# A selective scan: the velocity made for two values of n per weight load, and the work on it ordered by pairs of n

## The reference

```python
xz = einsum("bld,ed->ble", x, in_w); xb, z = split(xz)
xb = silu(causal_conv4(xb) + cb)
delta, Bm, Cm = split(einsum("ble,re->blr", xb, xp_w))     # 16, 16 and 16 columns
delta = softplus(delta @ dtw.T + dtb)
dA = exp(delta[..., None] * -exp(a_log))
mi = delta[..., None] * Bm[:, :, None, :] * xb[..., None]
# over time, for every channel e and state n:
v = 0.6 * v + mi_t
h = dA_t * h + v
y_t = sum over n of h * C_t
# and then
out = einsum("bld,ed->...", (y + dp * xb) * silu(z), ow)
```

## Time and profile before

| | us |
|---|---|
| runs | 4443.35, 4444.9, 4454.01 |
| median | 4444.9 |
| profiled execution, its span | 4448.6 |
| TensorE busy (PE) | 3574.1, 80% |
| VectorE busy (DVE) | 2793.3, 63% |
| ScalarE busy (ACT) | 1980.3, 45% |
| GpSimd busy (POOL) | 2081.9, 47% |

### The profile page before, as it was taken

One profiled execution on the slowest core, in us unless ns is written; L12 is line 12 of the kernel. 1 busy time (PEld: TensorE's weight loads), 2 busy tenths in 40 slices (PEclk: granted clock), 3 DMA queues, 4 the chain that ended last, 5 costly groups with the idle time before them and its releaser, 6 DMA issues. The chain is left out here.

```text
span 4448.6 us, 88475 instructions
## 1 busy us (share of the span) xinstructions
PE 3574.1 (80%) x28540; PEld 2392.4 (54%) x28541; DVE 2793.3 (63%) x4863; ACT 1980.3 (45%) x4454; POOL 2081.9 (47%) x1206
## 2 busy tenths in 40 slices
PE   6888869936988889888875888888988884499980
PEld 4454546624555555555543555555555553388870
DVE  3444432345777777777755777777777776655545
ACT  1212112205656666566634666656666553233320
POOL 0101000014667666676652766667667675422216
PEclk8888878967999999999986999999999995599995
DMA  1000000011313222132221221312223224211113
GB/s 50 0 0 0 0 21 0 0 56 41 74 51 73 52 54 74 49 75 52 53 63 33 64 61 51 76 50 60 66 51 73 51 55 152 99 48 47 47 40 109
DMA packets 151619, 230.36 MB, mean 52 GB/s; under 512 B 25106, under 2 KB 83890, under 8 KB 149556
## 3 DMA queue, kind: packets, MB, share of 16 engines
q1 hardware_dynamic: 143156, 202.30, 17.1%
q0 software_dynamic: 8064, 23.08, 1.8%
HBM read 119.99 MB, written 23.59 MB: 32 GB/s over the span
## 5 line engine op out<-in xcount | busy, mean ns | idle before, releaser
L893 POOL TENSOR_TENSOR m_hc<-m_h,m_Cb 128x1024 f32<-128x1024 f32 x512 | 1204.9, 2354 | 766.3 <-DVE m_h L1014 446.9
L1014 DVE TENSOR_TENSOR_SCAN m_h<-m_dA,m_hlast,m_bank 128x256 f32<-128x256 f32 x2048 | 1354.3, 725 | 145.3 <-PE m_bank L1295 62.6
L1277 PE MATMUL m_bank<-m_hc,ident 128*128 128x512 f32 x2048 | 1210.2, 680 | 147.9 <-POOL m_hc L893 147.6
L1144 ACT ACTIVATE m_dA<-m_delta,m_rate 128x256 f32<-128x256 f32 x2048 | 894.1, 500 | 16.3 <-DVE m_h L1014 15.4
L1293 PEld LDWEIGHTS m_bank<-m_M,m_U 128*128 128x128 bf16 x8192 | 605.1, 101 | 362.4 <-DVE m_h L1014 223.8
L1293 PE MATMUL m_bank<-m_M,m_U 128*128 128x64 bf16 x8192 | 675.2, 197 | 128.5 <-DVE m_h L1014 118.8
L1295 PEld LDWEIGHTS m_bank<-m_M,m_U 112*128 112x128 bf16 x8192 | 578.5, 100 | 205.6 <-issue 173.3
L1295 PE MATMUL m_bank<-m_M,m_U 112*128 112x64 bf16 x8192 | 675.3, 197 | 0.0
L1277 PEld LDWEIGHTS m_bank<-m_hc,ident 128*128 128x128 f32 x2048 | 337.8, 205 | 197.0 <-POOL m_hc L893 164.5
L962 DVE SCALAR_TENSOR_TENSOR m_cv<-m_xpre,m_conv,m_cv 128x256 f32<-128x256 f32 x384 | 272.3, 750 | 22.7 <-ACT m_cv L1082 18.2
L1207 PE MATMUL m_bank<-m_pair,m_in 128*128 128x256 f32 x1024 | 267.7, 388 | 7.6 <-ACT m_cv L1082 3.8
(11 more groups left out here) (273 smaller groups left out, 5637.6 us busy)
## 6 DMA issues: line engine op xcount, KB each, us to landing
m_Cb<-m_c_rows SPq DMA_DIRECT2D x256, 256.0 KB, 3.2
m_M<-m_Mhi SPq DMA_DIRECT2D x128, 256.0 KB, 4.1
m_M<-m_Mlo SPq DMA_DIRECT2D x64, 256.0 KB, 3.9
m_U<-m_Uhi SPq DMA_DIRECT2D x128, 128.0 KB, 3.2
y_rows<-x_y SPq DMA_DIRECT2D x40, 256.0 KB, 2.1
m_U<-m_Ulo SPq DMA_DIRECT2D x64, 128.0 KB, 3.4
g_stage<-in_e_w SPq DMA_DIRECT2D x8, 1024.0 KB, 5.4
o_stage<-in_e_w SPq DMA_DIRECT2D x16, 512.0 KB, 4.7
```

Source lines behind the costliest of these rows:

```text
L893: nc.gpsimd.tensor_tensor(hc[:, n % 2], h[:, n % RING], Cb[:, g % 2, n % NG, :].unsqueeze(1).broadcast_to([P, KI, CM]), ALU.mult).then_inc ...
L1014: nc.vector.tensor_tensor_scan(h[:, n % RING, m, :], dA[:, n % RING, m, :], VB[(n % 2) * 2 + g][:, (m % 2) * CM:(m % 2 + 1) * CM], hlast[: ...
L1144: nc.scalar.activation(dA[:, n % RING, m, :], delta[:, par, m, :], ACT.Exp, scale=rate[:, m, n:n + 1]).then_inc(s["da_done"], 1)
L1277: last = nc.tensor.matmul(Y[half][:], net.ident[:], hc[:, n % 2, 2 * half:2 * half + 2, :], start=(n == 0), stop=(n == NS - 1))
```

## The change

The velocity of one slot is made for one channel block m and two values of n (NG = 2): the moving operand is 128 columns wide (64 tokens of two n), and a bank holds one channel block for a pair of n. A slot is then (pair p, block m), with p = at // 4 and m = at % 4, where it was (n, half g). The scans, decays, products and sums follow that order: a scan slot has two scans, of the same block for two n; a product takes two blocks and two n; the sums add to Y0 from even products and to Y1 from odd ones, two matmuls each; keep_last copies a pair of n at a time, every fourth slot, and the last copy of a chunk moves into the next chunk's slot 1. ScalarE's first two chunks are written out before its loop. The buffers keep their sizes.

```diff
-RING, LEAD, OFF, NG = 4, 2, 10, 2
+OFF, NG = 10, 2
+HALF = 2 * NS
+NPAIR = NS // NG
...
-        dA = sb("dA", [P, RING, KI, CM])
-        h = sb("h", [P, RING, KI, CM])
+        dA = sb("dA", [P, 2, KI, NG, CM])
+        h = sb("h", [P, 2, KI, NG, CM])
         hlast = sb("hlast", [P, NS, KI])
-        hc = sb("hc", [P, 2, KI, CM])
+        hc = sb("hc", [P, 2, 2, NG, CM])
...
-                        sp.wait_ge(s["v_psum"], 1 + (c + 1) * NS * 2)
+                        sp.wait_ge(s["v_psum"], 1 + (c + 1) * HALF)
...
-                def product(c, par, n, next_scan=1):
-                    k = c * NS + n
-                    g = n // NG
-                    pool.wait_ge(s["scan_done"], 1 + AHEAD + (k + 1) * KI + next_scan)
-                    pool.wait_ge(s["acc_done"], 1 + AHEAD + k - 1)
-                    if n % NG == 0:
-                        pool.wait_ge(s[f"c_spread{g % 2}"], 1 + 16 * (c * (NS // NG // 2) + g // 2 + 1))
+                def product(c, k, next_scan=1):
+                    p, g = k // 2, k % 2
+                    at = c * NS + k
+                    pool.wait_ge(s["scan_done"], 1 + AHEAD + (at + 1) * KI + next_scan)
+                    pool.wait_ge(s["acc_done"], 1 + AHEAD + at - 1)
+                    if g == 0:
+                        pool.wait_ge(s[f"c_spread{p % 2}"], 1 + 16 * (c * (NPAIR // 2) + p // 2 + 1))
                     pool.sem_inc(net.carrier, 1)
-                    nc.gpsimd.tensor_tensor(hc[:, n % 2], h[:, n % RING],
-                                            Cb[:, g % 2, n % NG, :].unsqueeze(1).broadcast_to([P, KI, CM]), ALU.mult
-                                            ).then_inc(s["hc_done"], 1)
+                    nc.gpsimd.tensor_tensor(hc[:, g].rearrange("p m a t -> p m (a t)"),
+                                            h[:, p % 2, 2 * g:2 * g + 2].rearrange("p m a t -> p m (a t)"),
+                                            Cb[:, p % 2].rearrange("p a t -> p (a t)").unsqueeze(1).broadcast_to(
+                                                [P, 2, NG * CM]), ALU.mult).then_inc(s["hc_done"], 1)
...
-                def scan(c, n, g):
-                    k = c * NS + n
-                    if g == 0:
-                        dve.wait_ge(s["hc_done"], 1 + AHEAD + k - RING + 1)
-                        dve.wait_ge(s["hlast_done"], 1 + AHEAD + k - RING + 1)
-                    dve.wait_ge(s["v_psum"], 1 + k * 2 + g + 1)
-                    for m in (2 * g, 2 * g + 1):
-                        dve.wait_ge(s["da_done"], 1 + k * KI + m + 1)
+                def scan(c, at):
+                    p, m = at // KI, at % KI
+                    k = c * HALF + at
+                    if m % 2 == 0:
+                        dve.wait_ge(s["hc_done"], 1 + AHEAD + c * NS + 2 * p + m // 2 - 3)
+                    if m == 0:
+                        dve.wait_ge(s["hlast_done"], 1 + AHEAD + c * NPAIR + p - 1)
+                    dve.wait_ge(s["v_psum"], 1 + k + 1)
+                    for a in range(NG):
+                        dve.wait_ge(s["da_done"], 1 + k * NG + a + 1)
                         nc.vector.tensor_tensor_scan(
-                            h[:, n % RING, m, :], dA[:, n % RING, m, :],
-                            VB[(n % 2) * 2 + g][:, (m % 2) * CM:(m % 2 + 1) * CM],
-                            hlast[:, n, m:m + 1], ALU.mult, ALU.add).then_inc(s["scan_done"], 1)
+                            h[:, p % 2, m, a, :], dA[:, p % 2, m, a, :], VB[m][:, a * CM:(a + 1) * CM],
+                            hlast[:, NG * p + a, m:m + 1], ALU.mult, ALU.add).then_inc(s["scan_done"], 1)
...
+                def decays(c, par, at):
+                    p, m = at // KI, at % KI
+                    k = c * HALF + at
+                    if at == 0:
                         act.wait_ge(s["delta_done"], 1 + c + 1)
+                    for a in range(NG):
+                        act.wait_ge(s["scan_done"], 1 + AHEAD + (k - 2 * KI) * NG + a + 1)
                         act.sem_inc(net.carrier, 1)
+                        nc.scalar.activation(dA[:, p % 2, m, a, :], delta[:, par, m, :], ACT.Exp,
+                                             scale=rate[:, m, NG * p + a:NG * p + a + 1]).then_inc(s["da_done"], 1)
+
+                def keep_last(c, p):
+                    act.wait_ge(s["scan_done"], 1 + AHEAD + (c * NPAIR + p + 1) * KI * NG)
                     act.sem_inc(net.carrier, 1)
-                    nc.scalar.copy(hlast[:, n, :], h[:, n % RING, :, CM - 1]).then_inc(s["hlast_done"], 1)
+                    nc.scalar.copy(hlast[:, NG * p:NG * p + NG, :], h[:, p % 2, :, :, CM - 1].rearrange("p m a -> p a m")
+                                   ).then_inc(s["hlast_done"], 1)
+
+                def slots(c, par, more, more2, first=False):
+                    for at in range(HALF):
+                        if at + KI < HALF:
+                            decays(c, par, at + KI)
+                        elif more:
+                            decays(c + 1, 1 - par, at + KI - HALF)
+                        if at % KI == 1 and at > KI:
+                            keep_last(c, at // KI - 1)
+                        elif at == 1 and not first:
+                            keep_last(c - 1, NPAIR - 1)
...
-                def accumulate(c, n, half):
...
+                def accumulate(c, k, a):
+                    p, g = k // 2, k % 2
+                    if a == 0:
+                        pe.wait_ge(s["hc_done"], 1 + AHEAD + c * NS + k + 1)
+                        if p == 0:
+                            pe.wait_ge(s["gate_done"], 1 + c * KI + 2 * g + 2)
+                    last = nc.tensor.matmul(Y[g][:], net.ident[:], hc[:, g, :, a, :],
+                                            start=(p == 0 and a == 0), stop=(p == NPAIR - 1 and a == NG - 1))
+                    if a == NG - 1:
                         last.then_inc(s["acc_done"], 1)
...
-                    pe.wait_ge(s["scan_done"], 1 + AHEAD + (k - 2) * KI + 2 * g + 2)
-                    bank = VB[(n % 2) * 2 + g]
-                    for m in (2 * g, 2 * g + 1):
-                        for j in range(NSUB):
-                            at = (m % 2) * CM + j * SUB
-                            nc.tensor.matmul(bank[:, at:at + SUB], U1[:, par, j, m * P:(m + 1) * P],
-                                             M1[:, par, j, n, :], start=True, stop=False)
-                            last = nc.tensor.matmul(bank[:, at:at + SUB], U2[:, par, j, m * P:(m + 1) * P],
-                                                    M2[:, par, j, n, :], start=False, stop=True)
+                    pe.wait_ge(s["scan_done"], 1 + AHEAD + (c * HALF + at - KI + 1) * NG)
+                    bank = VB[m][:].rearrange("p (a t) -> p a t", a=NG)
+                    for j in range(NSUB):
+                        to = bank[:, :, j * SUB:(j + 1) * SUB]
+                        nc.tensor.matmul(to, U1[:, par, j, m * P:(m + 1) * P],
+                                         M1[:, par, j, NG * p:NG * p + NG, :], start=True, stop=False)
+                        last = nc.tensor.matmul(to, U2[:, par, j, m * P:(m + 1) * P],
+                                                M2[:, par, j, NG * p:NG * p + NG, :], start=False, stop=True)
                     last.then_inc(s["v_psum"], 1)
```

More of the change, by code:

```diff
@@ L921, in _ @@
                 slots(NCM - 1, 1, False, False)
-                product(NCM - 1, 1, NS - 1, 0)
+                product(NCM - 1, NS - 1, 0)
                 tail(NCM, 1, 3)
@@ L1019, in slots @@
                 def slots(c, par, more, more2):
                     restart()
-                    for n in range(NS):
-                        for at in (2 * n, 2 * n + 1):
-                            scan(c, n, at % 2)
-                            tail(c, 1 - par, at)
-                            if more:
-                                head(c + 1, 1 - par, at + OFF)
-                            if more2 and at + OFF >= 2 * NS:
-                                head(c + 2, par, at + OFF - 2 * NS)
+                    for at in range(HALF):
+                        scan(c, at)
+                        tail(c, 1 - par, at)
+                        if more:
+                            head(c + 1, 1 - par, at + OFF)
+                        if more2 and at + OFF >= HALF:
+                            head(c + 2, par, at + OFF - HALF)
@@ L1170, in _ @@
                     head(1, 1, at)
-                for n in range(LEAD):
-                    decays(0, 0, n, 0)
-                    decays(0, 0, n, 1)
-                with act.Fori(0, NCM // 2 - 1) as c2:
+                for at in range(KI):
+                    decays(0, 0, at)
+                slots(0, 0, True, True, True)
+                slots(1, 1, True, True)
+                with act.Fori(1, NCM // 2 - 1) as c2:
                     slots(c2 * 2, 0, True, True)
@@ L1185, in _ @@
                 for half in range(2):
```

(31 more changed lines are left out.)

70 lines of the change are left out of this document (7 added, 63 removed).

## The result

| | median, us | lowest to highest | ratio to the kernel before, 95% interval |
|---|---|---|---|
| before (4 runs) | 4449.45 | 4443.35 to 4462.9 | |
| changed (4 runs) | 4406.19 | 4400.95 to 4414.19 | 0.9908 [0.9883, 0.9933] |
| changed, second series (6 runs; before 4444.58) | 4403.14 | 4398.84 to 4413.18 | 0.9900 [0.9884, 0.9916] |

The change makes the kernel about 1% faster, 41 to 43 us. The forecast was 4408 us, 37 us less than before.

The account below looks back on a forecast made before the run. The prediction took TensorE to bound the long stretch before the gate and part of an earlier one, with GpSimd taking over there. Velocity -31 us and copies -6 us gave -37 us from 4444.9: 4408 us, range 4380 to 4436.

Parts of the forecast that it names:

- What bounds: Per chunk: TensorE sets the long stretch before the gate and the first part of an earlier one, then GpSimd takes over.
- the stretch to 1897: 22.0 us of the profiled chunk, TensorE without a hole; half its 9.25 slots counted, those before GpSimd takes over.
- The velocity: TensorE's velocity matmuls: 8 of 128 columns replace 16 of 64, about 57 ns apart, saving 0.05 us per slot.
- The sums over n: TensorE's two 512-column matmuls per product, now reading two runs of 256: cost 0.
- The slots: Slots where TensorE's saving counts: 14.75 plus half of 9.25, 19.4 of 32 per chunk, giving 31 us.
- The copies: ScalarE's last-column copies halve, 16 to 8 per chunk; two of 0.09 us on the path, 6 us gained.
- The added wait for a copy at every fourth slot: VectorE needs ScalarE's copy three slots after it instead of five; it comes in time, cost 0.
- The sum: Whole kernel: -31 us from velocity and -6 us from copies make -37 us, forecasting 4408 us.
- The split output: Slower rival: velocity output in two runs of 64 slows the matmuls, +307 us, about 4750 us; chance 0.04.
- Covered: Rival: GpSimd's products and VectorE's scans absorb TensorE's saving, under 13 us gained, 4432 to 4445 us; chance 0.17.
- The load showing: Slower rival: velocity weight loads follow one another at 0.07 us, +46 us, 4491 us; chance 0.03.

Follow-up runs that it names:

- low_cut: Changed kernel with GpSimd making only 64 of 1024 elements of the first low part of M per chunk; 4401.16 us, 0.9905 of the kernel before.
- narrow: Changed kernel with each velocity matmul cut into two of 64 columns, a weight load each, order by pairs kept; 4444.3 us, 0.9997 of the kernel before.
- copies16: Changed kernel with the last column of a pair copied in two instructions, 16 copies per chunk; 4406.93 us, 0.9910 of the kernel before.
- adjacent: Changed kernel with each piece's velocity written to 128 adjacent columns instead of two runs of 64; 4407.45 us, 0.9912 of the kernel before.
- last_wide: Changed kernel with velocity pieces 0 to 2 made by 64-column matmuls, only the last piece by 128-column ones; 4433.94 us, 0.9972 of the kernel before.
- one_more: Changed kernel with one more 128-column velocity matmul and its load in every slot; 0.9961 of the kernel before.
- mhi_later: Changed kernel with ScalarE's high parts of M made after the softplus, GpSimd's low parts following later; 4387.81 us, 0.9866 of the kernel before.
- sums_odd: Changed kernel with both matmuls of a product's sum over n issued back to back in the odd slot; 4401.9 us, 0.9900 of the kernel before.
- one_less: Changed kernel without the second velocity matmul of piece 0, 7 instead of 8 per slot; 0.9865 of the kernel before.
- last_narrow: Changed kernel with velocity pieces 0 to 2 made by 128-column matmuls, the last piece by four of 64; 4437.5 us, 0.9980 of the kernel before.

## Why the prediction was right, point by point

- **What bounds.** Right in the main: the 1.2 us per chunk came from TensorE's slot, and the gain lies in the long stretch before the gate. Wrong in the reason for the middle: the forecast let GpSimd's back-to-back work take over the stretch to 1897. low_cut moved u by 0.9 us on average, but not VectorE's delta, which waits for ScalarE's logarithm in both; ScalarE's chain without idle time leads up to it. GpSimd's work does hold up u, though. The chunk's 79.6 us in the prediction are a window that ends 1 us behind the next gate; from gate to gate that chunk has 78.43 us. That 79.7 is the mean of the 26 chunks made the forecast of about 78.5 us come out.
- **The velocity.** The spacing was forecast at 56 to 58 ns and is 58.5; the saving was taken as 0.05 us and is 0.040.
- **The sums over n**, costed at 0, gave 0.027 us per slot. This is the term that was missed. The sum behind another sum still takes 0.86 us, so reading in two runs cost nothing; the sum got cheaper because the identity's load starts with the last velocity matmul, and a longer last matmul covers more of it.
- **The slots.** 19.4 of 32 were counted; narrow gives 19.2. So the velocity and the sum make 0.067 x 19.2 x 32 = 41 us instead of 31. The agreement is luck in good part. The count held 4.6 slots ahead of the output's addition, where nothing was gained (21.3 us in both kernels). Behind u there are 14.0 slots; at 0.067 us they give 0.94 us of the 1.2 us by which that part got shorter, and TensorE's holes there shrank by 0.2 us. And one factor for all sizes of a slot's time does not exist, as the table of slots shows.
- **The copies.** 6 us forecast, nothing seen: narrow has fewer copies and the time of the kernel before to 0.16%, and in copies16 the 0.09 us of a copy are gone before u. The added wait for a copy at every fourth slot is part of narrow too and shows no cost there.
- **The sum.** -31 - 6 = -37 us against -41 to -43: one term too small by 10 to 12, one too large by 6. The two errors went against each other, and that the sum came within 6 us is luck in part.
- **The rivals.** The split output is refuted by adjacent. (The range 4380 to 4436 left out most of the rival Covered, 4432 to 4445, and not only its end.) The load showing is refuted by the spacing of 58.5 ns; by the Trainium skill (TensorE: Matmul & The Clock Gate, Back-to-back issue gap) it would have been about 81. Covered: that was true of the chunk up to u, not of the whole.

Left open: why 0.03 us more in last_wide costs as much as 0.056 us more in one_more. The granted clock is one candidate. In one chunk of low_cut it moved by enough to eat 0.7 us, and over 26 chunks TensorE's time at half clock is 12.1 to 12.2 us per chunk in the changed kernel and in last_wide, but 10.8 us in one_more. At half speed that would put about 0.65 us per chunk, 20 us, to one_more's credit.

The clocks of all runs say the same with smaller figures. Among the 17 runs of the kernel before beside narrow, those granted 0.868 took 4456 to 4457 us and the one granted 0.875 took 4432 us, some 3.6 us for each 0.001. That is how time and clock go together, not a proof of which moves which. An estimate from it, by the mean clock of the runs of each kernel against the changed one (0.869): one_more (0.873) has a credit of some 15 us, mhi_later (0.872) of 10 us, while low_cut (0.864) has lost 18 us, sums_odd (0.866) 10 us and one_less (0.866) 9 us. last_wide and last_narrow (both 0.869) have neither. So the clock would explain about half of what sets one_more apart, most of why low_cut and sums_odd gained nothing, and more than half of mhi_later's gain; of one_less it explains a part. The kernel before and narrow were granted 0.871 and the changed kernel 0.869, so the change's own 41 us are no gift of the clock; without that difference they would by the same estimate be some 6 us more. No run changed the clock by itself, so all of this stays a candidate.

## What to carry to other kernels

A matmul's listed duration overlaps the next; count by starts, and price a narrower or wider matmul from the starts of two widths in the same trace. The matmul ahead of the load of a float32 identity covers it for as long as that matmul takes (0.03 or 0.06 us here), so put the widest one last. Where an engine's chain of own work sets a part of the loop, take out of it what nobody waits for soon: mhi_later, which only moves four steps to later slots, was worth more than a third of the whole change. And compare the granted clock along with the time: in this kernel it moved with the edits, by as much as the effects that were looked for.

## What was not expected of the hardware

- The load of the float32 identity starts with the last bf16 matmul ahead of it, never earlier, and within 3 ns in nearly all of some 850 places of each trace: 0.939 us for the sum behind 64 columns, 0.912 us behind 128, whatever stands before the last one.
- Time won ahead of a stretch at low clock was lost in it in one chunk: 0.8 us earlier on GpSimd, a granted clock of 0.56 instead of 0.83 behind it, and the gate at the same place.
- The kernel's time is not linear in the work added to TensorE's slot: +0.030 us per slot cost 32 us, +0.056 us cost 27 us.
